# Four batches of convolution rows fetched on ACT's DMA queue instead of SP's

## The reference, cut to what matters

```python
# layer 0: a small attention over 8 block sums per batch gives one row per batch (proj),
# layer norm of x + proj, then a feed-forward with ternary weights and int8-rounded activations
h = silu(bitlinear(y, w1)) * bitlinear(y, w2)        # y: 4096 x 512, h: 4096 x 2048
x = x + bitlinear(h, w3)                             # 4096 x 512, called x1 below
# layer 1: a causal convolution along the 256 tokens of each batch,
# 16 taps per channel, the taps being cond_2048 (16 x 512)
z = conv(x, w)
logits = z @ Wr                                      # 8 experts
w, sel = top_k(logits, 2); w = softmax(w)
out = x + sum over the two chosen experts of w * (z @ We[e] + be[e])
```

## Time and profile before

| | |
|---|---|
| median of 3 runs | 964.23 us (963.39 to 965.83) |
| the profiled execution | 967.5 us, its span 965.7 us |
| PE busy | 767.3 us (79%) |
| DVE busy | 604.7 us (63%) |
| POOL busy | 539.7 us (56%) |
| ACT busy | 341.1 us (35%) |
| SP's hardware queue | 47.3% of the 16 DMA engines' span |

### The profile page before, as it was taken

The page is one execution under the profiler, slowest core; times in us unless marked ns, Lnnn a source line. Parts: engine busy times, 40 slices in busy tenths (PEclk is TensorE's granted clock), DMA queues, the critical chain, the costliest instruction groups (busy, mean ns, idle before and its releaser), DMA issues.

```text
span 965.7 us, 11684 instructions
## 1 busy us (share of the span) xinstructions
PE 767.3 (79%) x3467; PEld 445.0 (46%) x3498; DVE 604.7 (63%) x895; ACT 341.1 (35%) x499; POOL 539.7 (56%) x758
## 2 busy tenths in 40 slices
PE   7734679999999999997979994037999999999800
PEld 3311234444444444443646441035777877787600
DVE  0157889999989999976271005997655655556500
ACT  0254656766666677662212003111111111111100
POOL 1018789888878888831060005355576787777610
PEclk9956989999999999999989997557999999999955
DMA  9936137799999656436986774414687888888849
GB/s 339 412 125 196 33 82 136 157 174 188 173 174 180 151 116 132 97 86 129 223 136 104 215 101 118 132 48 103 111 149 133 155 156 151 144 147 165 139 102 280
DMA packets 214045, 147.13 MB, mean 152 GB/s; under 512 B 146256, under 2 KB 178000, under 8 KB 212576
## 3 DMA queue, kind: packets, MB, share of 16 engines
q1 hardware_dynamic: 197600, 104.13, 47.3%
q0 software_dynamic: 16128, 38.05, 21.9%
q10 hardware_dynamic: 256, 4.19, 1.4%
HBM read 89.19 MB, written 44.56 MB: 139 GB/s over the span
## 4 chain that ended last, share of the span: by engine, by line
PE 38%; DMA 15%; DVE 13%; POOL 13%; issue 9%; ACT 4%; SPq 4%; POOLq 0%; DVEq 0%; ACTq 0%
DMA x_scratch<-YS,IDS 11%; PE PS L1313 7%; PE PS L1264 7%; PE PS L1330 6%; PE PS L1285 6%; PE PS L1274 6%; POOL x_scratch L718 5%; PE PS L1216 3%; DMA QyT<-Qy 3%; PE PS L1373 2%; POOL ZR L711 2%; SPq L417 1%; DVE BD L1033 1%; DVE BOH L1134 1%; DVE YS L1197 1%
## 5 line engine op out<-in xcount | busy, mean ns | idle before, releaser
L1373 PE MATMUL PS<-W,ZH 128*128 x576 | 189.6, 411 | 5.8 <-DVE ZL L1182 4.9
L718 POOL DMA_INDIRECT x_scratch<-YS,IDS x72 | 119.2, 1655 | 67.4 <-SPq L534 38.7
L1264 PE MATMUL PS<-W,QyT 128*128 128x512 bf16 x502 | 123.4, 387 | 33.9 <-DMA QyT<-Qy 23.1
L1285 PE MATMUL PS<-W,QT 128*128 128x512 bf16 x499 | 117.8, 386 | 11.0 <-DVE W L890 6.2
L850 ACT CAST ZH<-PS 128x512 fp32r<-128x512 f32 x72 | 42.2, 587 | 237.5 <-PE PS L1357 206.0
L1274 PE MATMUL PS<-W,QyT 128*128 128x512 bf16 x504 | 121.5, 382 | 0.4
L1373 PEld LDWEIGHTS PS<-W,ZH 128*128 128x128 f32 x576 | 106.0, 193 | 29.0 <-issue 9.9
L1373 PE MATMUL PS<-W,ZL 128*128 x288 | 115.1, 400 | 0.0
L1197 DVE TENSOR_TENSOR YS<-PS,BEB 128x512 f32<-128x512 f32 x72 | 49.7, 691 | 104.0 <-DMA x_scratch<-YS,IDS 72.3
L779 ACT ACTIVATE SG<-PS,sm 128x1024 f32<-128x1024 f32 x64 | 71.1, 1110 | 72.4 <-PE PS L1264 72.4
L1264 PEld LDWEIGHTS PS<-W,QyT 128*128 128x128 bf16 x512 | 49.7, 99 | 97.6 <-DMA QyT<-Qy 25.9
(11 more groups left out here) (202 smaller groups left out, 1129.4 us busy)
## 6 DMA issues: line engine op xcount, KB each, us to landing
XW<-x_scratch SPq DMA_DIRECT2D x64, 240.0 KB, 4.9
X<-in_x SPq DMA_DIRECT2D x8, 1024.0 KB, 13.3
x_scratch<-X SPq DMA_DIRECT2D x32, 256.0 KB, 3.2
z_scratch<-ZZ SPq DMA_DIRECT2D x16, 512.0 KB, 13.1
WRAW<-in_We SPq DMA_DIRECT2D x8, 1024.0 KB, 9.3
XR<-in_x SPq DMA_DIRECT2D x20, 256.0 KB, 3.8
stage<-in_w1T SPq DMA_DIRECT2D x4, 1024.0 KB, 14.9
stage<-in_w2T SPq DMA_DIRECT2D x4, 1024.0 KB, 21.9
```

The lines of the kernel that those rows point to most:

```text
L718: pool.indirect_dma_start(x1_d, bass.IndirectOffsetOnAxis(IDS[:, m:m + 1].bitcast(U32), 0), YS[m % UN][:], None, compute_op=ALU.add).then_ ...
L1264: i = nc.tensor.matmul(GP[:, a, :], QyT[t][:, k, :], W12[:, k, o:o + CH], start=(k == 0), stop=(k == KD - 1))
L1285: i = nc.tensor.matmul(DN, QT[t][:, k, :], W3[:, k, :], start=(k == 0), stop=(k == KF - 1))
L1373: x = nc.tensor.matmul(bank[i], zz[i % 2][:, k, :], W2[:, bass.ds(q, 1), part, k, :].rearrange("p o d -> p (o d)"), start=(k == 0 and n == ...
```

## The change

`load_xw` moves out of SP's program and takes the issuing engine as an argument. SP's `stage(NT)` no longer fetches batches 8 to 11. ACT does, two batches at the head of its `stage(NT)` and two at the head of its `stage(NT + 1)`, each time after a wait for the last up projection. Batches 0 to 7 and 12 to 15 stay with SP. The number, the shapes and the semaphores of the transfers are the same.

```diff
+        def load_xw(eng, b):
+
+            for t in range(TB):
+                eng.wait_ge(x1_out[t], 16 * b + 16)
+            for j in range(NQ):
+                q, o = QD * j, b * S * D + j * NI
+                eng.dma_start(XW[q:q + QD, b * CB + 1:b * CB + CB, :],
+                              bass.AP(x1_d.tensor, o, [[D, QD], [OB * D, CB - 1], [1, NI]])).then_inc(xw_in[2 * b // B], 16)
+                eng.dma_start(XW[q + OB:q + QD, b * CB, :],
+                              bass.AP(x1_d.tensor, o, [[D, OB], [1, NI]])).then_inc(xw_in[2 * b // B], 16)
+
...
@@ SP, stage(s)
-                    sp.wait_ge(u_done, NH * NT)
-                    for b in range(B // 2, B - 4):
-                        load_xw(b)
...
             sp.wait_ge(down_done, NT)
-            load_xw(B - 4)
-            load_xw(B - 3)
+            load_xw(sp, B - 4)
+            load_xw(sp, B - 3)
             sp.wait_ge(x1_done, NT)
-            load_xw(B - 2)
-            load_xw(B - 1)
+            load_xw(sp, B - 2)
+            load_xw(sp, B - 1)
...
@@ ACT, stage(s)
             def stage(s):
+                if NT <= s <= NT + 1:
+                    act.wait_ge(u_done, NH * NT)
+                    load_xw(act, B // 2 + 2 * (s - NT))
+                    load_xw(act, B // 2 + 2 * (s - NT) + 1)
                 if tile(s):
                     silu(s, 0)
```

More of the change, by code:

```diff
@@ L407, in load_xr @@
                 sp.dma_start(XR[:, n % RING, :], x.rearrange("b s d -> (b s) d")[n * P:n * P + P, :]).then_inc(xr_in[n % RING], 16)
[L409 to L418, removed]
             def turn_y(n):
@@ L473, in stage @@
                 if s % TB == 0 and 4 <= s < B + 4:
-                    load_xw((s - 4) // TB)
+                    load_xw(sp, (s - 4) // TB)
                 if s == NT:
```

## The result

The changed kernel takes 977.4 us (median of 4 runs, 973.96 to 980.4) against 964.72 us for the kernel before (median of 4, 963.39 to 965.83): a ratio of 1.0136, 95% interval 1.0113 to 1.0159. It is slower by 1.4%, about 13 us. The forecast was 4.7 us slower, with a range up to 972.6; the sign was right, the size was not, and the time lies outside the range. The profiled execution took 973.96 us, its span 972.2.

A forecast was written before the change was run, and what follows sets the result against it. No engine alone was taken to bound the kernel; a relay on the last tile did. Issue delay 3.2, transposes 1.5, clock 0 and fetch gain 0 made +4.7 us on 964.2: 968.9 us, range 964.4 to 972.6.

The forecast's parts named there:

- issue term: ACT, before tile 31's casts: 16 DMA issues outlast the 5.3 us gap, delaying the casts 2.7 to 3.9, taken 3.2 us.
- transpose term: Tile 31's transposes, before the down projection: ACT's load backlog delays them; bounds -0.2 and +3.0, taken +1.5 us.
- rival 2: Tile 31's transposes held much longer, both queues perhaps taking turns in issuing; 3.9 + 3.0 + 2.0 = 8.9 us, chance 0.19.
- worth of early rows: Half of the convolution: 2.98 us XW wait goes, BD wait becomes about 6.8 us; gain 0.
- rival 4: Half of the convolution: transfers, not POOL, slow BD's copies; early rows save 6.8 us, 962.1 us in all; chance 0.08.
- Clock: PE's down projection of tile 31 after longer idling: bounds -1.7 to +2.0 us, taken as 0.

The follow-up runs named there:

- second_group_late: Changed kernel, but ACT issues batches 10 and 11 only once both transposes of tile 31 have landed; 972.97 us, ratio 1.005.
- issues_only: Kernel before, XW loads left on SP, plus 16 and 16 small DRAM-to-DRAM DMAs issued on ACT at the change's places; 974.62 us, ratio 1.0081.
- behind_casts: Changed kernel with all four batches on ACT issued right behind the two casts of tile 31; 971.1 us, ratio 1.0045.
- wrx_early: Kernel before, all XW loads on SP, with SP's eight WRX loads one stage earlier; 967.64 us, ratio 1.0001.
- before_wb: Kernel before with POOL's four WB multiplies each held until a further group's BD is built; 962.96 us, ratio 0.9952.
- behind_transposes: Changed kernel with all four batches on ACT issued once both transposes of tile 31 have landed; 969.78 us, ratio 1.0041.

## Why the prediction was right in sign and wrong in size

**The issue term held.** The casts were to come 3.2 us late. From the origin they come 444.13 - 438.73 = 5.40 us against 2.33: 3.1 us. The sixteen issues took 8.3 us, 0.52 each, and began while the last square ran. (The low bound of this term, 444.1 - 441.48, is 2.6 and not 2.7, which changes little.)

**The transpose term failed.** The step was: "I take +1.5, since the backlog is short", and with it the sentence that eight matmuls cover the second transpose "unless it is held 1.5 us more than the first". I counted what was left of the first eight pairs and passed over the second eight, although I wrote that the second transpose "now meets the next 16 loads". In the changed kernel the first transpose costs 4.35 us more (452.88 - 445.20 = 7.68 from its issue to PE's start, before 3.33), and the second holds the down projection 1.9 us longer (7.2 for 5.3, 1.71 of it waiting). 3.07 + 4.35 + 1.9 = 9.3 us, all of the shift in the first profile. `second_group_late` takes only that group away and has 1.7 us in place of the 4.35, near the forecast's 1.5. So what came is the outcome of rival 2, at 0.19, transposes held much longer. Of its mechanism, turns in the issuing, `issues_only` shows 1.0 and 0.5 us; the rest comes from the loads in flight. (The second transpose's issue did grow to 3.75 us, but in the trace of before one already took 3.17, on a single queue with loads ahead of it.) And rival 2 too was too small: its 3.0 us came from the longest landing of the trace of before, in which loads and transposes share one queue. That bound was not a bound for two queues.

**Why a second queue matters.** Wherever ACT's loads were in flight beside the transposes, these were slow (5.3 and 8.1 us in `behind_casts`, 7.5 and 11.6 in the changed kernel). Two things are mixed in that. Loads issued ahead of a transpose delay it on one queue too, up to 6.2 us. Loads issued behind it did not on one queue: in the trace of before five transposes had up to three loads behind them and none ahead, landed after 3.0 to 3.4 us, and none was overtaken, as in `wrx_early`. On ACT's queue three loads overtook the second transpose. How the second one's 8.5 us divide between loads ahead and loads behind is not shown; a run with as many loads behind the transposes on SP's queue was not made. In the time of the transposes ACT's queue had 84.2% share to SP's 40.8%. The prediction had the rule of the Trainium skill, "DMA: Bandwidth & Descriptors", section "Queues, rings and completion order", that the engines take turns between queues, and read it as a relief. The trace agrees with turns, but shows them as a cost: loads issued 0.4 to 1.5 us behind the second transpose landed 1.0 to 3.2 us ahead of it. I read the rule for the backlog alone.

**The worth of early rows was right.** No XW wait, one BD wait of 7.07 (forecast 6.8), PE going on 11.65 us after the first half as before; confirmed by `wrx_early`, and its cause, named against rival 4, by `before_wb`. The changed kernel's own trace speaks against rival 4 too: its last load of XW landed at 483.6, and from 484 to 498 us the DMA engines had a share of 0.00, yet the copies that began at 498.02 took 11.58 us together.

**Clock.** Taken as 0. The down projection's matmuls took 3.57 + 1.90 = 5.5 us, before 5.3. Fair for this trace, but see below.

**What stays open.** The later start of the convolution explains 9.3 and 11.1 us in two profiles; the measured difference is 13.1 (10.9 to 15.3) and 10.6 (8.9 to 12.4). The 11.1 lie in both intervals, the 9.3 in the second alone. The experts' stage varies by 3.5 us between profiles without a visible cause, 277.3 to 280.8 over all ten traces. Whether it is a little longer on average behind a late convolution I can't say.

## What to carry to other kernels

Before moving loads to a second DMA queue, look at what is in flight or is issued shortly after on the first. In these traces the order on one queue kept the loads behind a critical transfer from overtaking it; with two queues they did overtake it. Count the issues that come ahead of compute instructions on the issuing engine, and compare them with the gap in which it waits. And look at what is late next before paying for an earlier transfer: here a single added wait on POOL gave 0.5%, and with it an earlier fetch that had been worth nothing gave almost another 0.5%.

## What the runs showed of the hardware that I had not expected

ACT's DMA issues begin while its last compute instruction still runs (435.81 in 435.74 to 436.78), so the instruction in progress does not delay them. The compute instruction behind them waits: the cast began at 444.13, when the last of the sixteen issues had ended at 444.08.

The length of an issue varied with its kind and with the load: 8 KB from DRAM to DRAM took 0.61 us, 8 KB into SBUF 0.5. With both queues loaded the latter took up to 2.1 us on ACT in the changed kernel and up to 3.5 on SP in `behind_transposes`, though one on SP took 2.08 before, too.

After nearly the same idle time of 3.1 us the same 16 matmuls of the down projection took 4.90, 5.28, 5.30, 6.48 and 6.50 us in five traces. The granted clock was 0.50 while they ran slowly and about 1.0 behind that; it was back at 0.99 from 448 us on in the shortest, and still at 0.50 until 451 in that of 6.48 us. That alone moves the start of the convolution by 1.6 us from one trace to another, about half of what this kernel's measurement can tell.
